# First key products in groups, first output ahead of the third batch's values, logits and output between the halves of the values

## What is computed

```
x = layernorm(x + rwkv_attention(x))     # time mixing with the shifted x, k, v, r = three 256x256 products,
                                         # a recurrence over time per channel, sigmoid(r) * wkv, product with Wo
x = layernorm(x + moe(x))                # 8 experts of width 176, top 2 of 8, softmax over the two
x = layernorm(x + linear_attention(x))   # 16 heads of 16, elu + 1 features
x = layernorm(x + ternary_mlp(x))        # weights rounded to -1, 0, 1; sigmoid(x W1) * (x W2), then W3
```

## Time and profile before

| | us |
|---|---|
| median of 3 runs | 400.77 |
| lowest, highest of the runs | 400.18, 407.91 |
| the profiled execution | 400.25 |
| its span, first to last instruction | 398.4 |
| TensorE, VectorE, ScalarE, GpSimd busy | 361.3, 292.1, 210.5, 137.4 |
| mean granted clock of TensorE | 0.975 |

### The profile page before, as it was taken

One profiled execution on the slowest core, in us unless ns is written; L12 is line 12 of the kernel. 1 busy time (PEld: TensorE's weight loads), 2 busy tenths in 40 slices (PEclk: granted clock), 3 DMA queues, 4 the chain that ended last, 5 costly groups with the idle time before them and its releaser, 6 DMA issues.

```text
span 398.4 us, 7791 instructions
## 1 busy us (share of the span) xinstructions
PE 361.3 (91%) x2440; PEld 323.8 (81%) x2440; DVE 292.1 (73%) x748; ACT 210.5 (53%) x483; POOL 137.4 (34%) x233
## 2 busy tenths in 40 slices
PE   8999999999598999999999847999999999999790
PEld 8999889998476877767777736999999999999680
DVE  6996999999974584895453264797879788876741
ACT  6664677668555333355335414556555564646451
POOL 4001077776717520030310268244536240311201
PEclk9999999999789999999999998999999999999986
DMA  7899411111234357533521131102021100000000
GB/s 224 299 307 243 145 55 41 40 55 54 75 99 133 120 176 247 147 105 101 153 81 53 54 92 54 53 2 81 10 73 33 48 29 0 28 2 26 0 28 26
DMA packets 28567, 35.79 MB, mean 90 GB/s; under 512 B 3696, under 2 KB 25712, under 8 KB 28272
## 3 DMA queue, kind: packets, MB, share of 16 engines
q1 hardware_dynamic: 19696, 21.78, 18.4%
q0 software_dynamic: 3072, 8.39, 6.6%
q10 hardware_dynamic: 5760, 5.12, 3.9%
HBM read 22.83 MB, written 12.45 MB: 89 GB/s over the span
## 4 chain that ended last, share of the span: by engine, by line
PE 49%; DVE 34%; issue 8%; ACT 4%; POOL 3%; DMA 1%; ACTq 0%; DVEq 0%; POOLq 0%
PE bank L414 19%; PE bank L558 10%; PE bank L579 8%; DVE st L1110 4%; PE bank L750 2%; PE bank L424 2%; PE bank L695 2%; PE bank L538 2%; PE bank L568 2%; DVE arena L1599 2%; DVE arena L1592 2%; DVE arena L1173 2%; DVE arena L1197 1%; DVE arena L1494 1%; ACT arena L1073 1%
## 5 line engine op out<-in xcount | busy, mean ns | idle before, releaser
L812 ACT ACTIVATE arena<-bank 128x256 f32<-128x256 f32 (+1 forms) x118 | 45.3, 422 | 40.1 <-PE bank L579 28.9
L1688 POOL TENSOR_TENSOR ve<-mv,eps 128x2 f32<-128x2 f32 x32 | 8.1, 252 | 158.8 <-DVE mv L1114 111.5
L558 PE MATMUL bank<-gu,arena 128*128 x156 | 52.6, 460 | 0.0
L817 ACT ACTIVATE arena<-arena,nm,rs 128x256 f32<-128x256 f32 x48 | 26.2, 596 | 39.8 <-POOL nm L1696 39.6
L1772 POOL DMA_INDIRECT arena<-yg,ypos x32 | 31.2, 974 | 38.9 <-DMA yg<-arena 30.4
L579 PE MATMUL bank<-dn,arena 96*128 x156 | 41.1, 385 | 2.4 <-DVE arena L1370 2.4
L1370 DVE COPY arena<-bank 96x256 f32<-96x256 f32 x39 | 16.3, 419 | 33.3 <-PE bank L568 32.9
L1742 POOL DMA_INDIRECT xg<-x,pos x32 | 35.4, 1107 | 14.3 <-issue 7.3
L579 PEld LDWEIGHTS bank<-dn,arena 96*128 96x128 f32 x156 | 28.6, 190 | 11.9 <-issue 4.3
L414 PE MATMUL bank<-arena 128*128 128x256 f32 (+2 forms) x192 | 34.3, 321 | 3.4 <-DVE arena L1185 1.9
L414 PE MATMUL bank<-x_hi,w1q 128*128 128x256 f32 x128 | 36.0, 305 | 1.5 <-ACT x_hi L812 1.5
(11 more groups left out here) (275 smaller groups left out, 1120.0 us busy)
## 6 DMA issues: line engine op xcount, KB each, us to landing
arena<-xg SPq DMA_DIRECT2D x39, 128.0 KB, 2.1
yg<-arena ACTq DMA_DIRECT2D x39, 128.0 KB, 1.7
arena<-in_xT SPq DMA_DIRECT2D x8, 256.0 KB, 5.9
x<-in_x SPq DMA_DIRECT2D x8, 256.0 KB, 4.5
out<-arena SPq DMA_DIRECT2D x8, 256.0 KB, 2.1
gu<-in_w_gate SPq DMA_DIRECT2D x1, 1408.0 KB, 9.7
gu<-in_w_up SPq DMA_DIRECT2D x1, 1408.0 KB, 13.8
dn<-in_w_down SPq DMA_DIRECT2D x11, 128.0 KB, 6.5
```

Of the source, the lines that this page charges most:

```text
L558: last = pe.matmul(bank[BANK_GU[i % 2]][:, 0:2 * F], xtT[:, i % 2, chunk(k)], w[:, :, k, :, bass.ds(e, 1), :], start=k == 0, stop=k == KC - 1)
L812: return act.activation(dst, src, ACT.Copy)
L817: last = act.activation(dst[:, t, :], src[:, t, :], ACT.Identity, bias=nm[:, i, t:t + 1], scale=rs[:, i, t:t + 1])
```

## The change

`WARM` goes from 16 to 11. The keys of batch 0 get a function of their own, `first_keys`, which runs the same 24 products in six groups of four, each behind a wait for just what it reads. ScalarE and VectorE split half of the key weights, then batch 0's input, then the other half. `xs_high(1)` and `xs_low(1)` move from the preparation into the stream of stage A. In TensorE's slots `logits` and `output` go between the two halves of the V product; in slot 1, where there are no logits yet, `output(0)` goes ahead of all of V. In the slots with an early rank it goes between the halves of R. The wait for `cv_ok` moves ahead of `turn_x1`.

```diff
-WARM = 16
+WARM = 11
...
-            def project(b, j, dst, done):
-                if j == 0:
+            def project(b, j, dst, done, parts=range(KC)):
+                if j == 0 and 0 in parts:
                     pe.wait_ge(xsl_ok, b + 1)
                 if b == 0:
-                    pe.wait_ge(wlow_ok, j + 1)
-                for d in range(KC):
+                    pe.wait_ge(wlow_ok, j + 2)
+                for d in parts:
...
-                last.then_inc(done, 1)
+                if KC - 1 in parts:
+                    last.then_inc(done, 1)
+
+            def first_keys(dst):
+                def add(w, x, k, first=False, final=False):
+                    for lag in range(2):
+                        for d in range(KC):
+                            last = pe.matmul(dst[:, d, :], w[0][:, lag * KC + k, chunk(d)],
+                                             x[0][:, k, 1 - lag:1 - lag + T],
+                                             start=first and lag == 0 and d == 0, stop=final and lag == 1,
+                                             skip_group_check=True)
+                    return last
+
+                pe.wait_ge(xsh_ok, 1)
+                pe.wait_ge(whigh_ok, 2)
+                add(wA_hi, xs_hi, 0, first=True)
+                pe.wait_ge(wlow_ok, 1)
+                add(wA_lo, xs_hi, 0)
+                pe.wait_ge(whigh_ok, 4)
+                add(wA_hi, xs_hi, 1)
+                pe.wait_ge(xsl_ok, 1)
+                add(wA_hi, xs_lo, 0)
+                add(wA_hi, xs_lo, 1)
+                pe.wait_ge(wlow_ok, 2)
+                add(wA_lo, xs_hi, 1, final=True).then_inc(kp_mm, 1)
...
             def a_slot(s):
                 old, now, new = s - 2, s - 1, s + 1
-                if 0 <= new < B:
+                value_bank = halves(1 + new % 2)
+                if new == 0:
+                    first_keys(halves(0))
+                else:
                     past(pe, ku_ok, new)
                     project(new, 0, halves(0), kp_mm)
-                if 0 <= old < B:
+                past(pe, cv_ok, new - 1)
+                if 0 <= old:
                     turn_x1(old)
-                if 0 <= new < B:
-                    past(pe, cv_ok, new - 1)
-                    project(new, 1, halves(1 + new % 2), vp_mm)
-                if 0 <= old < B:
+                    project(new, 1, value_bank, vp_mm, (0,))
                     logits(old)
-                if 0 <= now < B - 1:
+                if 0 <= now:
                     output(now)
+                project(new, 1, value_bank, vp_mm, range(1 if 0 <= old else 0, KC))
                 if old == FULL_AT - 1:
                     rank(old)
                     first_total()
-                if 0 <= new < B:
-                    past(pe, gate_ok, new)
-                    project(new, 2, halves(3), rp_mm)
+                past(pe, gate_ok, new)
+                project(new, 2, halves(3), rp_mm, (0,))
                 if 0 <= old < FULL_AT - 1:
                     rank(old)
+                project(new, 2, halves(3), rp_mm, (1,))
...
-            weights_high(0)
+            weights_high(0, (0,))
             xs_high(0)
+            weights_high(0, (1,))
             weights_high(1)
             weights_high(2)
-            xs_high(1)
...
             for s in range(-1, B - 1):
                 a_slot(s)
+                if s == -1:
+                    xs_high(1)
...
-            weights_low(0)
+            weights_low(0, (0,))
             xs_low(0)
+            weights_low(0, (1,))
             weights_low(1)
             weights_low(2)
...
-            xs_low(1)
...
                 exponents(s)
+                if s == 0:
+                    xs_low(1)
                 differences(s)
```

More of the change, by code:

```diff
@@ L825, in _, with weights_high @@
             act.wait_ge(unmix_ok, 1)
-            def weights_high(j):
+            def weights_high(j, parts=range(KC)):
                 act.wait_ge(in_kvr[j], 16)
-                for k in range(KC):
+                for k in parts:
                     act.activation(wA_hi[j][:, k, :], raw_kvr[:, j, k, :], ACT.Copy,
@@ L1134, in _, with weights_low @@
             dve.wait_ge(unmix_ok, 1)
-            def weights_low(j):
+            def weights_low(j, parts=range(KC)):
                 dve.wait_ge(in_kvr[j], 16)
-                for k in range(KC):
+                for k in parts:
                     dve.wait_ge(whigh_ok, 2 * (KC * j + k) + 1)
```

## The result

| | before | after |
|---|---|---|
| median of the runs (5 each) | 400.77 | 398.11 |
| lowest, highest | 400.15, 407.91 | 397.15, 398.85 |
| the profiled execution | 400.25 | 397.15 |
| its span | 398.4 | 395.1 |
| mean granted clock | 0.975 | 0.970 |

The ratio is 0.9932, with a 95% interval from 0.9905 to 0.9958: 2.7 us faster by the medians, 3.1 by the two profiled executions. Every ratio in this text leaves out the runs that took over 1.5% longer than the fastest of their kernel, such as the 407.91 here, while the medians keep them.

What follows compares the result with a forecast made beforehand. TensorE bounds the kernel before about 33 us and after 106, VectorE between. Start-up -0.38, output -2.90, slot 6 +0.7 make -2.6; with the clock's -0.6, 400.25 less 3.2 is 397.05; forecast 397.3, range 395.0 to 400.3.

Steps and rivals of the forecast that it cites:

- First keys: Start-up: keys in groups and a shorter warm-up start the keys 1.48 us earlier on TensorE, putting VectorE 0.38 ahead.
- The sign of being wrong that named this load: Stage A: the prediction called itself wrong if `xs_low(3)` waits for its load, batch 3's xT.
- `output(0)` ahead of V: Slot 1: with the output before batch 2's values, VectorE's whole 2.90 us wait before `residual(0)` goes, with 1.0 of cover.
- the bound stated without the start-up: Slot 1: with no gain in the start-up, output ready at 30.0 and 2.8 us of the wait still gone.
- Some of its slack is used up: Beginning K of batch 3, TensorE is only 1.4 us ahead while VectorE is 3.28 ahead, so TensorE loses slack.
- Slots 2 to 5: Logits and output between V's halves only displace idle time: 0 gained, covered by 0.2 us at logits, 0.7 at rank.
- The cover given for the rank: Slots 2 to 5: rank near 74.2 again, read by VectorE at 75.55, given as 0.7 us of cover.
- Slot 6: V's second half between `output(5)` and `rank(4)` makes `positions(4)` later: +0.7 us, bounds 0.3 and 1.1.
- The clock: Granted clock, from 100 us on: the low stretch may end somewhat sooner as seen from the work, -0.6 us.
- the clock gives more: Rival, chance 0.20: the clock's fall on the last block goes, -1.8 us beside the -3.2, giving 395.5.
- TensorE too late by a little: Rival, chance 0.18: VectorE waits 0.4 us in each of four slots, so only -1.0 in all, giving 399.3.
- slower: Rival, chance 0.05: TensorE's slot grows above VectorE's, `rank` arriving late; with 1.1 us per slot the kernel takes 402.

Runs made afterwards that it cites:

- e4_warm16: The changed kernel with WARM back at 16 in place of 11; 397.85 us, ratio 0.9925 to the kernel before.
- a2_changed_again: The changed kernel run once more with nothing edited, on a slower chip; 405.40 us, ratio 0.9985 to the kernel before.
- e5_rank_behind_R: The changed kernel with rank back behind all of R in slots 2 to 5, V still in halves; 400.04 us, ratio 0.9972 to the kernel before.
- e1_output_alone: The kernel before with only output(0) moved ahead of batch 2's value products in slot 1; 398.35 us, ratio 0.9938 to the kernel before.
- e6_rank4_first: The changed kernel with rank(4) and first_total ahead of V's second half in slot 6; 399.17 us, ratio 0.9962 to the kernel before.
- e3_no_halves: The changed kernel with V and R whole again in slots 2 to 6, output(0) still ahead of V; 397.73 us, ratio 0.9937 to the kernel before.
- e8_warm6: The changed kernel with WARM at 6 in place of 11, on a slower chip; 406.89 us, ratio 1.0005 to the kernel before.
- e7_pairs_on_gpsimd: e6_rank4_first with the constants of pairs() made on GpSimd in the start-up instead of on VectorE; 395.88 us, ratio 0.9888 to the kernel before.
- e10_pairs_no_halves: e7_pairs_on_gpsimd with V and R whole again in slots 2 to 6, on a slower chip; 404.47 us, ratio 0.9903 to the kernel before.
- e11_early_load: e7_pairs_on_gpsimd with batch 2's xT load issued ahead of six others, on a slower chip; 403.01 us, ratio 0.9943 to the kernel before.

## Why the prediction was right, step by step

1. **First keys: right.** TensorE 1.53 earlier (forecast 1.48), `exponents(0)` 0.87 (0.85), VectorE 0.41 at the differences and at `finish_y(0)` (0.38). The argument that ScalarE's other weights, and not the keys, hold `keys(0)` is shown by e4_warm16: 0.6 later keys, the same scan. The load for batch 3 was issued at 14.09 (forecast 14.2) and its DMA row says 9.5 us to landing, so 23.6, within the cover in this execution; in a2_changed_again it landed at 25.3 and cost 0.15. The sign of being wrong that named this load was thus met in part there: `xs_low(3)` itself came 0.02 later, and the scan behind it 0.14. The two prices for it were 24.1 (it slips with its issue) and 23.3 (it stands behind what was issued ahead of it, by the Trainium skill, DMA: Bandwidth & Descriptors, Queues, rings and completion order); the measured one lies between, and one landing of batch 2's load can differ from the next by 2.6, so this doesn't decide between them. **What the step missed** is batch 2's load. I looked at the one whose issue the change delays and not at this one, for which ScalarE's `xs_high(2)` waited 0.63 already before, 0.24 in this execution and 2.74 in e5_rank_behind_R, and whose margin to VectorE is as thin as the other's. It cost nothing in the profile shown and up to 1.1 in others.

2. **`output(0)` ahead of V: right.** `residual(0)` has no wait and starts at 29.44 (forecast 29.56). e1_output_alone confirms the bound stated without the start-up: 2.8 forecast, 2.83 at `residual(0)`. "Some of its slack is used up" also came true there: 0.5 lost in slot 2. In the changed kernel the start-up's lead pays for it.

3. **Slots 2 to 5: right, at 0.** No wait of VectorE, slots of 12.7, logits and rank at their old places on VectorE's clock. The cover given for the rank (0.7) was about the right size: e5_rank_behind_R, with another half of R (1.45) ahead of it, waits 0.58, so 0.87 were covered; it waits in two of four slots, and not in all four, because a slot in which VectorE waited gives the next one time.

4. **Slot 6: the mechanism right, the size wrong.** +0.7 was predicted, +0.25 measured (3.44 ahead at `residual(5)`, 93.82 against 97.26; 3.19 at `positions(4)`). Two terms were off by much. The room for V's second half ahead of `rank(4)` was taken from the bracket of the earlier trace rows, 0.54. But a bracket on TensorE counts from a modelled end. TensorE's timeline of the kernel before, logits and output of slot 6:

```profile
93.85 2.78 PE L414 MATMUL bank<-arena 128*128 128x8 f32 x16
```

   By starts, logits and output take 92.57 - 90.11 = 2.46, and before the rank came 97.17 - 93.85 = 3.32 behind the logits: room of 0.86. With 1.64 for V's half (forecast 1.55) and the 0.30 by which the logits do start earlier, the rank is 1.64 - 0.86 - 0.30 = 0.48 late, which is what the trace has (94.21 against 97.17 - 3.44 = 93.73). The Trainium skill (Perfetto Trace Analysis, Tensor Engine Instruction) says so in general: the end of a product is estimated by the profiler; these two numbers show what it is worth here, 0.32. And VectorE read the rank 0.78 after its start before, while 94.76 - 94.21 = 0.55 is enough: 0.23 of slack, which I had left out. e6_rank4_first and e3_no_halves give the 0.25 back, so the place is shown.

5. **The clock: wrong, at -0.6.** Behind `output(6)` the kernel took 291.64 against 291.75: -0.1. The falls on `output(6)` and on the last block stayed on the same products (3.78 for the one, 3.54 against 1.91 for the other). The term was an estimate from two rows, and it should have been zero with a wide range: in the runs here, falls come and go between executions of kernels that differ by nothing near them, and between two of the same kernel (a2_changed_again). The rival "the clock gives more", with no fall on the last block, did occur, in the executions of e3_no_halves and e8_warm6; since these two edits have nothing to do with that block, I take it for a draw and not for an effect of the change.

The sum by the trace is -0.41 - 2.90 + 0.25 = -3.06, and -3.19 at `output(6)`; the remaining 0.13 lies in small differences, 0.09 of it where 28.74 + 1.20 = 29.94 was taken for VectorE's arrival and the next instruction in fact starts 1.11 behind the scan's start. The profiled execution met the forecast of -3.2 by luck, through two errors that cancel: slot 6 too dear by 0.45, the clock too good by 0.5. The medians moved by 2.7. The rivals: "TensorE too late by a little" and "slower" had their signature in slots 2 to 5, and there is no wait there in this execution, nor is `xs_low(3)` late.

## What to carry to other kernels

Where a wait goes, ask with what margin the next one is met and who else reads at that place: here the output's move used up TensorE's slack in slot 2, and start-up and halves each cover it. As a cover either looks worthless when it alone is taken out, and not when both are (0.5) or when VectorE gets faster (0.9). Count the cost of a piece put between two TensorE operations from start to start, not from the idle time in a bracket, and subtract the reader's own slack. And once the named wait is gone, read what the bounding engine does instead: the constants it computed in passing were worth 1.3 us in the trace, where the whole change gained 3.2.

## What the runs showed of the hardware

- **The first rise of the clock** varies by more than expected. TensorE's timeline of e5_rank_behind_R, whose preparation is that of the changed kernel:

```profile
6.24 1.22 PE L444 MATMUL bank<-xT_hi,kv_hi 128*128 128x256 f32 x4
7.26 0.69 PE L444 MATMUL bank<-xT_hi,kv_lo 128*128 128x256 f32 x4
```

  Its first four products take 1.02 where the changed kernel's took 0.57, and in e6_rank4_first the same 22 records of the warm-up were over 0.8 sooner (4.21 us). In all, the traces record 2.4 GHz from a first time between 4.4 and 7.5 us into the span with 11 or 16 in the warm-up, and from 11.0 with 6. (The clock column of the windows has nothing to go by ahead of that time and says 1.00 there; the pace of the products shows the lower level.) The Trainium skill (TensorE: Matmul & The Clock Gate, What you observe) gives 500 ns either way; here it was 1.5 us either way. VectorE's start hung on it in no run but the one with 6.
- **Later falls** are not a property of the kernel alone: seen at 53.6, 129 and 148 us in one execution each and at 127 in three, beside those near 103, 235 and 377 us that nearly all have. One on critical products cost 0.9 to 1.9 us.
- **A load of 256 KB in a full stretch of DMA** took 5.3 us in one execution and 8.1 in another, issued at about the same time behind the same loads. Batch 3's load took 9.5 and 11.2 in two executions of the same kernel. A margin under 2 us on such a load is none.
- **GpSimd's small additions** took 0.2 to 1.1 us each in e7_pairs_on_gpsimd (twenty from 10.25 to 21.8), and VectorE's instructions of 128x510 and 128x512 beside them stayed at 0.65 to 0.70. The Trainium skill (Perfetto Trace Analysis, Optimizing Scalar/DVE Operations) warns that work moved between these two engines may not help, as they share a port; here 1.34 us of VectorE's path went away, at little cost: a first `exponents` of 0.76 in place of 0.69 in that trace, of 0.78 in e10_pairs_no_halves. In e11_early_load one GpSimd addition took 1.9 us and one of VectorE's instructions beside the additions 0.81 in place of 0.69, and the first scans of slots 0 and 1 are 10.26 apart in place of 10.08. That the port is the cause is not shown.
